# Projections of a graph-attention layer: from duos with seven products to trios with fifteen

## The chip, the cores and the metric

The kernel runs on one core of a Trainium2 chip (trn2). The metric is the time of one execution on the device, in microseconds (us). TensorE (PE) multiplies matrices and writes to PSUM; VectorE (DVE), ScalarE (ACT) and GpSimd (POOL) work on SBUF and PSUM; SyncE (SP) issues DMAs. Each engine runs its own instructions in order and waits on semaphores of the others.

## The reference

6250 nodes have 512 features each; 106250 edges, sorted by their destination, join them (self loops are among them). With eight heads of 64:

```python
Q, K, V = x @ Wq, x @ Wk, x @ Wv                       # 512 x 512 each
score = exp(clip(sum_d(K[src] * Q[dst]) / 8, -5, 5))   # per edge and head
h = x + segment_sum(V[src] * score, dst) / (segment_sum(score, dst) + 1e-6)
h = (h - mean(h, 0)) * rsqrt(var(h, 0) + 1e-5) * gamma + beta
out = layernorm(x + h)                                 # over the features
```

All in float32, output included.

## The kernel before, in words

The nodes lie in 49 tiles of 128 rows (the last is partly empty). Three stages follow one another. `project` computes Q, K and V of every tile and stores K and V side by side as rows of `kv_d`, and Q, split into a high and a low part, as rows of `q_d`. `attend` gathers the rows of `kv_d` by the edges' sources (indirect DMAs from POOL, line 751), multiplies them with Q, takes exponentials and sums by destination. `normalise` does the rest. Every gather needs all of `kv_d`: before its first one POOL waits for every store of K and V (`s_kva`, `s_kvb`).

Only `project` changes. Its core multiplies two tiles at a time (a duo): the product of the duo's x (two row blocks, the 512 inputs cut in two halves) with the weights (1536 columns cut in two halves of 768) is a product of 2 by 2 by 2 blocks, done in seven block products and sums (Strassen's method in Winograd's form). One block product is four `matmul` calls of 512 or 256 columns (the trace shows two MATMULs for one call). `product` on PE makes them (line 342); the sums of x blocks are made by DVE in `x_sums` (lines 480 to 485), those of the weights once in `weight_sums` (467 to 473); DVE and ACT decode the results out of PSUM (u2, u3, u4, kv_a, kv_b, c21; lines 590 to 616 and ACT's 435, 440). `split` (491, 493) makes the high part of Q with a scaling and the low part with a subtraction. There are 23 such duos (g = 0 to 22). The last duo's tiles (46, 47) and the 49th tile (`LONE`) are multiplied plainly (line 402: four `matmul` calls of 512 columns for one tile and one matrix, eight MATMULs in the trace); K and V of `LONE` come first of all (357, 374), its Q last.

What sets the order is written out by hand: every engine's list of instructions with its waits. `s_prod` counts finished products, `s_sums` the x sums, `s_wt` the weight sums, `s_split` the parts of Q. x is loaded three duos deep.

Besides, DVE computes tables of the edges piece by piece (`tables(n)`, one piece n after each of three places of a duo): pieces 0 to 6 count visits (497, 498), piece 20 releases POOL (`s_cnt`), pieces 21 to 27 make the digits (503), for each of which ACT writes a row (428). POOL, once released, adds beta to the 49 tiles of x: load (314), add (323, `xb`), store (331). At g = 12 PE transposes the source indices (365), and DVE copies them out (587).

## Time and profile before

| | us |
|---|---|
| median of 3 runs | 1910.76 (1909.86 to 1912.99) |
| the profiled execution | 1908.01 |
| its span | 1906.1 |
| PE / DVE / ACT / POOL busy in the span | 1861.6 / 1697.0 / 1367.5 / 1291.3 |
| PE's first product starts at | 10.47 |
| last copy of K and V ends at | 449.65 |
| first gather issued at | 452.53 |

The page shows the busy time of each engine in 40 slices of 47.65 us; `project` is the first nine and a half. TensorE's granted clock is shown per slice. The page's idle times name who ended the wait.

### The profile page before, as it was taken

The page shows a single profiled execution, that of the slowest core. Times are in us where ns is not written, and L with a number is a line of the kernel's source. Part 1 is how long each engine was busy: PE and PEld are TensorE (multiplying, and loading weights), DVE is VectorE, ACT ScalarE, POOL GpSimd, SP SyncE. Part 2 cuts the span into 40 slices and gives each one's busy share as a digit, 9 for nine tenths or more (in the row PEclk, how much of TensorE's full clock was granted, in tenths as well). Part 3 has the DMA queues.
Part 4 walks back from the last instruction along what each step waited for, and adds up shares of the span by engine and source line. Part 5 has one row for each costly group of instructions (what it writes and reads, how often), then busy time and mean ns, then how long its engine had stood idle before and what let it go on. Part 6 is the DMA issues. An engine that isn't in the chain of part 4 may idle for free.

```text
span 1906.1 us, 41424 instructions
## 1 busy us (share of the span) xinstructions
PE 1861.6 (98%) x7904; PEld 1362.2 (71%) x8014; DVE 1697.0 (89%) x2454; ACT 1367.5 (72%) x4602; POOL 1291.3 (68%) x1473
## 2 busy tenths in 40 slices
PE   7999999998999999999999999999999999999897
PEld 4555555554888888878888888888888888887333
DVE  6677755644999999999999999999999999999888
ACT  0002000002999999999999999999999999998857
POOL 0205666103777888788888888888888888885677
PEclk9999999999999999999999999999999999999999
DMA  5547788546999999999999999999999999999307
GB/s 183 162 151 250 288 319 274 186 161 231 357 358 356 362 367 358 346 351 368 368 356 353 352 366 369 354 355 355 366 361 358 360 355 365 370 358 370 122 33 287
DMA packets 184521, 589.09 MB, mean 309 GB/s; under 512 B 28480, under 2 KB 30240, under 8 KB 184480
## 3 DMA queue, kind: packets, MB, share of 16 engines
q0 software_dynamic: 135904, 465.14, 65.8%
q1 hardware_dynamic: 45120, 121.69, 17.8%
q10 hardware_dynamic: 3456, 1.78, 0.3%
q8 instruction: 18, 0.29, 0.1%
q14 instruction: 23, 0.19, 0.0%
HBM read 535.27 MB, written 78.91 MB: 322 GB/s over the span
## 4 chain that ended last, share of the span: by engine, by line
PE 74%; DVE 16%; issue 4%; DMA 4%; ACT 1%; POOL 1%; SPq 0%; DVEq 0%; ACTq 0%; POOLq 0%
PE acc L939 29%; PE places L342 22%; PE q_ps L923 17%; DVE kv L795 6%; DVE raw L806 5%; DMA kv<-kv_d,idx 2%; PE mm_ps L949 2%; PE banks L1151 1%; DVE stats L1288 1%; DVE agg L1281 1%; PE mm_ps L951 1%; PE places L402 1%; DMA q_tile<-xb_d 1%; POOL kv L751 1%; PE banks L1142 1%
## 5 line engine op out<-in xcount | busy, mean ns | idle before, releaser
L751 POOL DMA_INDIRECT kv<-kv_d,idx x880 | 887.0, 1008 | 339.2 <-issue 204.8
L846 ACT ACTIVATE kv<-kv 128x64 f32<-128x64 f32 x3520 | 889.0, 335 | 14.3
L939 PE MATMUL acc<-kv,mm_sb 128*128 128x260 f32 x3520 | 845.6, 383 | 4.1 <-POOL kv L714 2.2
L939 PEld LDWEIGHTS acc<-kv,mm_sb 128*128 128x128 f32 x3520 | 654.3, 190 | 137.9 <-issue 32.8
L923 PE MATMUL q_ps<-q_tile,mm_sb 128*128 x1760 | 559.2, 439 | 5.6 <-DVE kv L795 4.9
L795 DVE TENSOR_TENSOR kv<-q_ps,kv 128x1024 f32<-128x1024 f32 x440 | 536.1, 1218 | 14.0 <-PE q_ps L923 7.0
L806 DVE TENSOR_REDUCE raw<-kv 128x16 f32<-128x1024 f32 x440 | 532.2, 1210 | 0.0
L923 PEld LDWEIGHTS q_ps<-q_tile,mm_sb 128*128 128x128 f32 x1760 | 328.6, 189 | 74.4 <-DVE kv L795 20.8
L714 DVE TENSOR_TENSOR kv<-kv 128x384 f32<-128x384 f32 (+1 forms) x440 | 271.6, 617 | 0.1
L857 ACT ACTIVATE mm_sb<-mm_ps,less 128x1024 fp32r<-128x1024 f32 x220 | 241.2, 1096 | 13.1 <-remote 10.1
L435 ACT COPY p<-places 128x768 f32<-128x768 f32 x23 | 18.4, 798 | 243.5 <-PE places L342 243.5
L342 PE MATMUL places<-t_sb,s_sb 128*128 128x512 f32 (+1 forms) x552 | 185.6, 486 | 0.0
L342 PEld LDWEIGHTS places<-t_sb,s_sb 128*128 128x128 f32 x552 | 104.8, 190 | 73.7 <-issue 66.7
L714 POOL TENSOR_TENSOR kv<-kv 128x128 f32<-128x128 f32 x220 | 139.7, 635 | 14.2 <-ACT kv L861 9.1
L861 ACT ACTIVATE kv<-raw 128x16 f32<-128x16 f32 x440 | 91.1, 207 | 53.3 <-DVE raw L799 49.7
L342 PE MATMUL places<-w_sb,x_sb 128*128 128x512 f32 (+1 forms) x368 | 126.2, 486 | 0.0
L342 PEld LDWEIGHTS places<-w_sb,x_sb 128*128 128x128 f32 x368 | 69.9, 190 | 49.1 <-issue 44.5
L949 PEld LDWEIGHTS mm_ps<-nb,lb 128*128 128x128 bf16 x880 | 67.5, 98 | 34.8 <-issue 2.2
L590 DVE TENSOR_TENSOR u<-places,p 128x768 f32<-128x768 f32 x23 | 22.0, 957 | 75.5 <-PE places L342 75.5
L949 PE MATMUL mm_ps<-nb,lb 128*128 128x128 bf16 x880 | 85.1, 219 | 1.5 <-ACT mm_sb L857 1.5
L440 ACT COPY kv_a<-places 128x256 f32<-128x256 f32 x23 | 8.6, 372 | 103.3 <-DMA kv_d<-kv_a 51.8
L799 DVE TENSOR_SCALAR raw<-raw 128x16 f32<-128x16 f32 x440 | 78.9, 179 | 0.0
(171 smaller groups left out, 1358.6 us busy)
## 6 DMA issues: line engine op xcount, KB each, us to landing
q_tile<-q_d SPq DMA_DIRECT2D x49, 512.0 KB, 7.2
kv<-kv_d,idx POOLq DMA_INDIRECT x880, 6.2
kv_d<-kv_a SPq DMA_DIRECT2D x25, 512.0 KB, 5.5
xb<-in_x POOLq DMA_DIRECT2D x49, 256.0 KB, 4.3
xb_d<-xb POOLq DMA_DIRECT2D x49, 256.0 KB, 3.7
out_rows<-agg SPq DMA_DIRECT2D x49, 256.0 KB, 2.1
x_sb<-in_xT SPq DMA_DIRECT2D x24, 512.0 KB, 7.9
q_d<-q_a SPq DMA_DIRECT2D x24, 512.0 KB, 4.1
```

What stands on the lines that cost most here:

```text
L342: last = pe.matmul(out[:, cols], left[:, c, :], right[:, c, cols], start=fresh and c == 0, stop=c == DEEP - 1, skip_group_check=True)
L714: return eng.tensor_tensor(v, v, w, ALU.mult)
L751: pool.indirect_dma_start(kv[:, s, u, 0:2 * DIM], None, kv_d, bass.IndirectOffsetOnAxis(idx[:, s, u:u + 1], 0), bounds_check=N_NODES - 1, ...
L795: dve.tensor_tensor(k, q_ps[:, :, :], k, ALU.mult).then_inc(s_mul[s], 1)
L799: dve.tensor_scalar(raw[:, s1, :, :], raw[:, s1, :, :], -5.0, 5.0, ALU.max, ALU.min).then_inc(s_clip[s1], 1)
L806: dve.tensor_reduce(raw[:, s, :, :], heads(kv[:, s, :, 0:DIM]), AX.X, ALU.add).then_inc(s_red[s], 1)
L846: return act.activation(v, v, ACT.Copy, scale=kv[:, s, u, 2 * DIM + h:2 * DIM + h + 1])
L857: act.activation(mm_sb[:, sa // 2, :, :], mm_ps[:, :, :], ACT.Relu, bias=less[:, 0:1]).then_inc(s_mm[sa // 2], 1)
L861: act.activation(kv[:, s, :, 2 * DIM:KVW], raw[:, s, :, :], ACT.Exp).then_inc(s_exp[s], 1)
L923: last = pe.matmul(q_ps[:, u, :], one_hot(sb_, u, 1), part_q, start=(n == 0), stop=(n == 1))
L939: last = pe.matmul(acc[:, bass.ds(par, 1), DIM - (1 - n) * HALF:DIM + n * HALF], m, kv[:, sc, u, DIM + n * HALF:DIM + (n + 1) * HALF], sta ...
L949: pe.matmul(mm_ps[:, 0, n * P:(n + 1) * P], lb[:, sa + n // 2, n % 2 * P:(n % 2 + 1) * P], nb[:, :], start=True, stop=True)
```

## The change

`project` works on three tiles at a time (a trio; g = 0 to 15 covers 48 tiles). x has three row blocks and two halves of its inputs, and the weights have two halves of their inputs and three column blocks (K's 512 columns, Q's and V's): a 3 by 2 by 3 block product, done in fifteen products of 512 columns (two `matmul` calls each, line 367 of the new kernel) instead of eighteen. The numbering of sums and products (X9, T9, BANK_9 and so on) is by product. The weights need eleven sums of 1024 columns instead of four of 1536, x eleven of 256 columns for a trio instead of four for a duo, and the decoding fourteen instructions of 512 columns on DVE (counted by `s_dec`) and six copies on ACT (`s_kc`). The five buffers u2, u3, u4, p1, c21 become seven places `c_sb` (`held`); K and V of a tile are stored apart, as halves of a row. x is held two trios deep instead of three duos, the x sums once instead of twice. `LONE` is done whole at the start, in the order K, Q, V (line 375). The first loads are issued in turn: x of `LONE` and Wk, then, when the first half of Wk has landed, Wq, x of the first trio and Wv; POOL's first load (`dl`) waits for the same half. The first products wait for each half of a matrix. The transposes of the indices are at g = 8, the digits (pieces 21 to 27) come in trios 7, 8 and 9: three, three and one.

```diff
+                elif g > 1:
+                    sp.wait_ge(s_prod, made(g - 2, 15))
+                sp.dma_start(x_sb[:, g % 2, :, :, :],
...
+            sp.dma_start(x_sb[:, 1, 0, :, :], xT[LONE]).then_inc(s_x[1], 16)
+            load_w(wk, 0, s_wk)
+            sp.wait_ge(s_wk[0], 16)
+            load_w(wq, 1, s_wq)
+            load(0)
+            load_w(wv, 2, s_wv)
             sp.wait_ge(s_kc, 1)
-            sp.dma_start(kv_d[LONE * P:(LONE + 1) * P, :], kv_a[:, :]).then_inc(s_kva, 16)
...
+            load(1)
...
+                if 0 < g < TRIOS - 1:
+                    load(g + 1)
...
+                a, b, c = 3 * g, 3 * g + 1, 3 * g + 2
+                sp.wait_ge(s_kc, copied(g, 4))
+                store_k(c, k_out(2), s_kva)
+                sp.wait_ge(s_dec, decoded(g, 3))
+                store_v(b, v_out(1), s_kvb)
+                store_q(a, split_of(g, 0), q_a, s_qa)
+                sp.wait_ge(s_dec, decoded(g, 7))
+                store_k(a, k_out(0), s_kva)
+                sp.wait_ge(s_dec, decoded(g, 8))
+                store_k(b, k_out(1), s_kva)
+                sp.wait_ge(s_dec, decoded(g, 11))
+                store_v(a, v_out(0), s_kvb)
+                sp.wait_ge(s_dec, decoded(g, 12))
+                store_v(c, v_out(2), s_kvb)
+                store_q(b, split_of(g, 1), q_b, s_qb)
+                store_q(c, split_of(g, 2), q_c, s_qc)
...
-            pool.dma_start(dl[:, :], dlast.broadcast_to([P, BLOCKS_IN])).then_inc(s_dl, 16)
...
+            pool.wait_ge(s_wk[0], 16)
+            pool.dma_start(dl[:, :], dlast.broadcast_to([P, BLOCKS_IN])).then_inc(s_dl, 16)
...
+                    last = pe.matmul(place(bank), left[:, c, :], right[:, c, :], start=fresh and c == 0,
+                                     stop=c == DEEP - 1, skip_group_check=True)
...
-                    pe.wait_ge(s_c22, g)
+                    pe.wait_ge(s_dec, decoded(g - 1, 14))
...
+                pe.wait_ge(s_x[g % 2], trio_x(g))
+                if g:
+                    pe.wait_ge(s_kc, copied(g - 1, 4))
+                product(BANK_5, a_part(g, 2, 0), weight(B00), True)
+                pe.wait_ge(s_sums, summed(g, X9))
+                wait(pe, s_dec, decoded(g - 1, 7))
+                first_wait(g, 2)
+                product(BANK_9, x_sum(X9), weight(T9), True)
+                pe.wait_ge(s_sums, summed(g, X2))
+                wait(pe, s_dec, decoded(g - 1, 8))
+                first_wait(g, 3)
+                product(BANK_2, x_sum(X2), weight(T2), True)
+                pe.wait_ge(s_kc, copied(g, 1))
...
+                pe.wait_ge(s_kc, copied(g, 2))
+                pe.wait_ge(s_sums, summed(g, X10))
+                first_wait(g, 4)
+                product(BANK_9, x_sum(X10), weight(T10), False)
...
+                pe.wait_ge(s_dec, decoded(g, 1))
+                first_wait(g, 7)
+                product(BANK_9, a_part(g, 0, 1), weight(T14), False)
...
                 if g == 0:
...
+                pe.wait_ge(s_sums, summed(g, X8))
+                pe.wait_ge(s_kc, copied(g, 6))
+                first_wait(g, 11)
+                product(BANK_1, x_sum(X8), weight(T8), False)
+                pe.wait_ge(s_sums, summed(g, X7))
+                wait(pe, s_dec, decoded(g - 1, 14))
+                if g == 0:
+                    pe.wait_ge(s_split, 2)
+                product(BANK_7, x_sum(X7), weight(B11), True)
...
+                wait(act, s_dec, decoded(g - 1, 8))
+                act.copy(held(M5), place(BANK_5)).then_inc(s_kc, 1)
+                act.wait_ge(s_prod, made(g, 2))
+                wait(act, s_dec, decoded(g - 1, 14))
+                act.copy(held(M9), place(BANK_9)).then_inc(s_kc, 1)
...
+                for landed in (*s_wk, *s_wq):
+                    dve.wait_ge(landed, 16)
+                dve.tensor_tensor(weight(T0), weight(B00), weight(B01), ALU.subtract).then_inc(s_wt, 1)
+                dve.wait_ge(s_prod, 2)
...
+                dve.tensor_tensor(weight(T1), weight(B02), weight(T0), ALU.subtract).then_inc(s_wt, 1)
+                dve.tensor_tensor(weight(T6), weight(B12), weight(T0), ALU.subtract).then_inc(s_wt, 1)
+                dve.tensor_tensor(weight(T8), weight(B11), weight(T13), ALU.add).then_inc(s_wt, 1)
+
+            def x_sums_first(g):
+                dve.wait_ge(s_x[g % 2], trio_x(g))
+                if g:
+                    dve.wait_ge(s_prod, made(g - 1, 6))
+                dve.tensor_tensor(x_sum(X9), a_part(g, 0, 0), a_part(g, 2, 0), ALU.add).then_inc(s_sums, 1)
+                dve.tensor_tensor(x_sum(X2), a_part(g, 1, 0), a_part(g, 2, 0), ALU.add).then_inc(s_sums, 1)
+                dve.wait_ge(s_sums, summed(g, X9))
+                dve.tensor_tensor(x_sum(X10), x_sum(X9), a_part(g, 0, 1), ALU.add).then_inc(s_sums, 1)
+                dve.wait_ge(s_sums, summed(g, X2))
+                dve.tensor_tensor(x_sum(X4), x_sum(X2), a_part(g, 1, 1), ALU.add).then_inc(s_sums, 1)
...
-            for g in range(LAST):
-                if g == TABLE_DUO:
+            x_sums_third(0)
+            x_sums_last(0)
+            dve.wait_ge(s_prod, 2)
+            split(q_c, place(BANK_7), 1, s_qc, 0)
+            for g in range(TRIOS):
...
+                dve.tensor_tensor(held(T), place(BANK_9), held(M5), ALU.subtract).then_inc(s_dec, 1)
...
+                dve.tensor_tensor(held(U), place(BANK_2), held(M5), ALU.add).then_inc(s_dec, 1)
                 tables(3 * g)
-                dve.wait_ge(s_prod, made(g, 3))
-                split(q_a, place(g, 0)[:, 0:DIM], 2 * g + 1, s_qa, 16 * g)
-                dve.wait_ge(s_prod, made(g, 4))
-                dve.wait_ge(s_u, 3 * g + 1)
-                dve.tensor_tensor(u3[:, :], place(g, 2)[:, 0:SIDE], u2[:, :], ALU.add).then_inc(s_u, 1)
-                if g + 1 < LAST:
-                    x_sums(g + 1)
+                dve.wait_ge(s_prod, made(g, 7))
+                dve.wait_ge(s_kvb, 16 * (1 + 3 * g))
+                dve.wait_ge(s_dec, decoded(g, 2))
+                dve.wait_ge(s_kc, copied(g, 5))
+                dve.tensor_tensor(v_out(1), place(BANK_13), held(U), ALU.subtract).then_inc(s_dec, 1)
+                dve.tensor_tensor(held(M13), held(M13), held(M9), ALU.add).then_inc(s_dec, 1)
+                dve.wait_ge(s_prod, made(g, 8))
+                dve.tensor_tensor(held(T), held(T), place(BANK_0), ALU.subtract).then_inc(s_dec, 1)
+                dve.wait_ge(s_dec, decoded(g, 5))
+                dve.tensor_tensor(held(M9), held(M9), held(T), ALU.subtract).then_inc(s_dec, 1)
+                split(q_a, held(T), split_of(g, 0), s_qa, 16 * g)
+                if g + 1 < TRIOS:
+                    x_sums_first(g + 1)
+                dve.wait_ge(s_prod, made(g, 9))
+                dve.wait_ge(s_kc, copied(g, 4))
+                dve.tensor_tensor(k_out(0), place(BANK_9), held(M5), ALU.subtract).then_inc(s_dec, 1)
...
                 tables(3 * g + 1)
...
+                if g + 1 < TRIOS:
+                    x_sums_second(g + 1)
+                dve.wait_ge(s_kc, copied(g, 6))
+                dve.tensor_tensor(held(M1), held(M1), held(M2), ALU.add).then_inc(s_dec, 1)
+                dve.tensor_tensor(held(M2), held(M2), v_out(1), ALU.add).then_inc(s_dec, 1)
+                dve.wait_ge(s_prod, made(g, 12))
+                dve.wait_ge(s_dec, decoded(g, 9))
+                dve.tensor_tensor(v_out(0), place(BANK_0), held(M1), ALU.add).then_inc(s_dec, 1)
+                dve.wait_ge(s_prod, made(g, 13))
+                dve.wait_ge(s_dec, decoded(g, 10))
+                dve.tensor_tensor(v_out(2), place(BANK_3), held(M2), ALU.subtract).then_inc(s_dec, 1)
                 tables(3 * g + 2)
...
+                dve.wait_ge(s_prod, made(g, 14))
+                dve.tensor_tensor(held(M13), place(BANK_1), held(M13), ALU.subtract).then_inc(s_dec, 1)
+                dve.wait_ge(s_dec, decoded(g, 13))
+                split(q_b, held(M13), split_of(g, 1), s_qb, 16 * g)
+                if g + 1 < TRIOS:
+                    x_sums_third(g + 1)
+                dve.wait_ge(s_prod, made(g, 15))
+                dve.wait_ge(s_split, 2 * split_of(g, 0))
+                dve.tensor_tensor(held(T), place(BANK_7), held(M9), ALU.add).then_inc(s_dec, 1)
+                dve.wait_ge(s_dec, decoded(g, 14))
+                split(q_c, held(T), split_of(g, 2), s_qc, 16 * (g + 1))
+                if g + 1 < TRIOS:
+                    x_sums_last(g + 1)
...
-            pool.wait_ge(soft["s_kva"], 16 * (TILES // 2 + 1))
-            pool.wait_ge(soft["s_kvb"], 16 * (TILES // 2 + 1))
+            pool.wait_ge(soft["s_kva"], 16 * TILES)
+            pool.wait_ge(soft["s_kvb"], 16 * TILES)
```

What DVE executes just before the copy of the transposed indices (the last row), from the decoding of c21 in duo 11 on; u3 and u4 are sums decoded into SBUF:

```order
L608 TENSOR_TENSOR c21<-u3,places 128x512 [waits s_prod]
L609 TENSOR_TENSOR kv_b<-u3,places 128x256
L491 TENSOR_SCALAR q_b<-c21 128x512 [waits s_qb,s_c21]
L493 SCALAR_TENSOR_TENSOR q_b<-c21,q_b 128x512 [waits s_split]
L616 TENSOR_TENSOR kv_a<-places,u4 128x768 [waits s_u,s_kva,s_prod]
L587 CAST src_t<-places 128x896 [waits s_tr]
```

And now, from the splitting of the second tile's Q in trio 7 on (`places` is PSUM, `c_sb`, `q_b`, `q_c`, `s_sb`, `x_sb` are SBUF):

```order
L565 TENSOR_SCALAR q_b<-c_sb 128x512 [waits s_qb,s_dec]
L567 SCALAR_TENSOR_TENSOR q_b<-c_sb,q_b 128x512 [waits s_split]
L551 TENSOR_TENSOR s_sb<-s_sb,x_sb 128x256 [waits s_sums,s_prod]
L552 TENSOR_TENSOR s_sb<-x_sb,s_sb 128x256
L553 TENSOR_TENSOR s_sb<-s_sb,x_sb 128x256
L554 TENSOR_TENSOR s_sb<-x_sb,s_sb 128x256
L714 TENSOR_TENSOR c_sb<-places,c_sb 128x512 [waits s_split,s_prod]
L565 TENSOR_SCALAR q_c<-c_sb 128x512 [waits s_qc,s_dec]
L567 SCALAR_TENSOR_TENSOR q_c<-c_sb,q_c 128x512 [waits s_split]
L559 TENSOR_TENSOR s_sb<-s_sb,x_sb 128x256 [waits s_prod]
L666 CAST src_t<-places 128x896 [waits s_tr]
```

Nine of the ten rows before the copy read SBUF alone, where two of five did. L714 is the last of the trio's fourteen decoding instructions, which the transposes of the next trio wait for.

PE around the transposes, before:

```order
L342 MATMUL places<-w_sb,s_sb 128x512
L342 MATMUL places<-w_sb,s_sb 128x256
L365 MATMUL places<-ident,kv 128x128 [waits s_c22,s_visit]
L365 MATMUL places<-ident,kv 128x128 x6
L342 MATMUL places<-w_sb,x_sb 128x512 [waits s_u,s_x0]
```

and now:

```order
L367 MATMUL places<-w_sb,s_sb 128x512 [waits s_dec,s_sums]
L367 MATMUL places<-w_sb,s_sb 128x512
L392 MATMUL places<-ident,kv 128x128 [waits s_dec,s_visit]
L392 MATMUL places<-ident,kv 128x128 x6
L367 MATMUL places<-w_sb,x_sb 128x512 [waits s_kc,s_x0]
L367 MATMUL places<-w_sb,x_sb 128x512
L367 MATMUL places<-w_sb,s_sb 128x512 [waits s_dec,s_sums]
```

The transposes waited for a result decoded after the fifth of the duo's seven products (`s_c22`); now they wait for the one decoded after the last of fifteen.

## Rows read from the trace of the kernel before

**Rows 1.** TensorE's granted clock in the page's 40 slices (tenths of full speed).

```profile
PEclk9999999999999999999999999999999999999999
```

**Rows 2.** The chain of waits to 460 us: start us, us, what.

```profile
10.47 5.17 PE places L357 x8
...
18.22 3.43 PE places L374 x8
21.66 214.14 PE places L342 x664
235.80 0.77 PE places L365 x7
236.56 198.73 PE places L342 x616
435.29 13.75 PE places L402 x32
...
449.06 0.59 ACT kv_b L450
...
459.18 10.32 DMA kv<-kv_d,idx
```

**Rows 3.** Timeline of DVE at the start: start us, us, line, shapes, idle before.

```profile
8.73 0.23 DVE L577 CAST iota_row<-iota_i 128x128 f32<-128x128 int32 x1 [6.50 <-DMA kv<-in_dlast]
...
9.71 1.02 DVE L581 TENSOR_TENSOR kv<-kv 128x832 f32<-128x832 int32 x1
...
13.94 0.42 DVE L483 TENSOR_TENSOR s_sb<-x_sb 128x256 f32<-128x256 f32 x1
14.28 0.42 DVE L485 TENSOR_TENSOR s_sb<-x_sb,s_sb 128x256 f32<-128x256 f32 x1
...
17.63 1.76 DVE L469 TENSOR_TENSOR t_sb<-w_sb,t_sb 128x1536 f32<-128x1536 f32 x1
```

**Rows 4.** Timeline of DVE in duo 22, when POOL is quiet.

```profile
432.75 0.69 DVE L608 TENSOR_TENSOR c<-u,places 128x512 f32<-128x512 f32 x1 [0.76 <-PE places L342]
433.35 0.41 DVE L609 TENSOR_TENSOR kv_b<-u,places 128x256 f32<-128x256 f32 x1
433.68 0.42 DVE L491 TENSOR_SCALAR q_b<-c 128x512 fp32r<-128x512 f32 x1
434.14 0.69 DVE L493 SCALAR_TENSOR_TENSOR q_b<-c,q_b 128x512 fp32r<-128x512 f32 x1
```

**Rows 5.** Groups by shape, DVE, 150 to 340 us: busy us, mean ns.

```profile
L493 DVE SCALAR_TENSOR_TENSOR q_b<-c,q_b 128x512 fp32r<-128x512 f32 x10 | 15.0, 1499 | 0.3
...
L483 DVE TENSOR_TENSOR s_sb<-x_sb 128x256 f32<-128x256 f32 x11 | 10.0, 909 | 0.0
...
L482 DVE TENSOR_TENSOR s_sb<-s_sb,x_sb 128x256 f32<-128x256 f32 x11 | 9.3, 842 | 0.4
...
L491 DVE TENSOR_SCALAR q_b<-c 128x512 fp32r<-128x512 f32 x10 | 6.4, 642 | 0.0
L480 DVE TENSOR_TENSOR s_sb<-x_sb 128x256 f32<-128x256 f32 x11 | 6.2, 567 | 0.0
```

**Rows 6.** Timeline of DVE and POOL at 272 us.

```profile
271.78 2.48 DVE L493 SCALAR_TENSOR_TENSOR q_b<-c,q_b 128x512 fp32r<-128x512 f32 x1
...
272.41 1.29 POOL L323 TENSOR_TENSOR xb<-xb,bet 128x512 f32<-128x512 f32 x1
```

**Rows 7.** Groups by shape, POOL, 150 to 350 us.

```profile
L323 POOL TENSOR_TENSOR xb<-xb,bet 128x512 f32<-128x512 f32 x49 | 63.1, 1287 | 4.4 <-DMA xb<-in_x 3.9
```

**Rows 8.** Groups by shape, DVE, 20 to 435 us: the digits.

```profile
L503 DVE TENSOR_SCALAR kv<-kv 128x1024 int32<-128x1024 int32 x7 | 5.5, 788 | 0.0
```

**Rows 9.** DMA issues of x from 234 and from 288 us: KB, us to landing.

```profile
x_sb<-in_xT SPq DMA_DIRECT2D x1, 512.0 KB, 9.6
...
x_sb<-in_xT SPq DMA_DIRECT2D x1, 512.0 KB, 13.2
```

**Rows 10.** Timeline at the first gather.

```profile
452.53 1.07 POOL L751 DMA_INDIRECT kv<-kv_d,idx  x1 [104.09 <-DMA kv_d<-kv_b]
```

More of the change, by code:

```diff
@@ L338, in _, with product @@
         def _(pe):
-            def product(out, left, right, fresh=True, told=True):
+            def product(bank, left, right, fresh):
                 for c in range(DEEP):
-                    for cols in (slice(0, DIM), slice(DIM, SIDE)):
-                        last = pe.matmul(out[:, cols], left[:, c, :], right[:, c, cols], start=fresh and c == 0,
-                                         stop=c == DEEP - 1, skip_group_check=True)
-                if told:
-                    last.then_inc(s_prod, 1)
@@ L347, in by_sum @@
-            def by_sum(g, n, k):
-                pe.wait_ge(s_sums, 4 * g + k)
-                wait(pe, s_wt, k if g == 0 else 0)
-                product(place(g, n), s_sb[:, g % 2, k - 1, :, :], t_sb[:, k - 1, :, :])
-            pe.wait_ge(s_x[X_DUOS - 1], 16)
-            lone = x_sb[:, X_DUOS - 1, 0, :, :]
-            pe.wait_ge(s_wk, 16 * CHUNKS)
-            for c in range(CHUNKS):
-                pe.matmul(place(-1, 5)[:, 0:DIM], lone[:, c, :], w_sb[:, c, DIM:2 * DIM], start=c == 0,
-                          stop=c == CHUNKS - 1)
@@ L387, in _ @@
+                first_wait(g, 10)
+                product(BANK_0, x_sum(X6), weight(T6), False)
+                pe.wait_ge(s_sums, summed(g, X3))
+                wait(pe, s_dec, decoded(g - 1, 12))
                 if g == 0:
                     pe.wait_ge(s_kc, 1)
[L389 to L394 removed]
@@ L395, in _ @@
-                pe.wait_ge(s_u, 3 * g + 1)
-                pe.wait_ge(s_sums, 4 * g + 4)
-                product(place(g, 5), s_sb[:, g % 2, 3, :, :], b_part(1, 1))
-            def plain(out, left, n):
-                for c in range(CHUNKS):
-                    last = pe.matmul(out, left[:, c, :], w_sb[:, c, n * DIM:(n + 1) * DIM], start=c == 0,
-                                     stop=c == CHUNKS - 1)
-                return last
-            a, b = (x_sb[:, LAST % X_DUOS, n, :, :] for n in range(2))
```

368 lines of the change are left out of this document (176 added, 192 removed).

## The prediction

> **What bounds the kernel now.** I read the chain of waits first. Up to 449.06 us it is TensorE (PE) alone: K of `LONE` from 10.47 us, then 83 block products in 214.14 us, the transposes in 0.77 us, 77 products in 198.73 us and the plain products in 13.75 us, with no gap that anyone else made [rows 2]. The granted clock is full in all slices [rows 1]. So `project` is as long as PE's columns take, and what counts is the moment at which the last part of K and V leaves PSUM: ACT's copy from 449.06 to 449.65 us. POOL's first gather starts at 452.53 us [rows 10], 2.9 us behind it, and the chain's first step that isn't PE's is a gather, 459.18 to 469.50 us [rows 2]. What follows (three quarters of the time) has the same instructions in both kernels; I take it as shifted as a whole by the shift of that moment. PE's own Q products behind it, three of 3.43 us before and two of 1.72 now, lie beside the stores and the gathers, and the chain doesn't run through them; so I count their saving as nothing (bounds: half of the 6.9 us gained, 2 us lost if the last stores of Q, closer to the gathers now, hold them up).
>
> The second reading is DVE's. Its instructions that read only SBUF take longer while POOL adds beta. The low part of Q takes 0.69 us when POOL is quiet [rows 4], and 1.50 us on average between 150 and 340 us [rows 5]; one of them, 2.48 us long, started 0.63 us before an addition of POOL's and ended 0.56 us behind it [rows 6]. POOL makes 49 additions of 1.29 us, none of which shows a delay on average [rows 7]. What reads PSUM isn't touched.
>
> **PE's work and the start.** A block product of 1536 columns takes 214.14 / 83 = 2.58 us, a plain one of 2048 takes 3.43 us [rows 2]; so one of 1024 takes 1.72 us, and a trio 15 x 1.72 = 25.8 us (8.6 us a tile, against 9.03). The first eight MATMULs took 5.17 us, 1.74 more than the later eight, after 10.5 us without work and at a granted clock shown as full [rows 1, 2]. I keep that. When PE starts is not in the trace: the first half of Wk now has 0.75 MB ahead of it or with it, where Wk shared the queues with 3 MB. At half of what was needed before I take 4.8 us (bounds 4 and 8, the latter near the old 10.47 less the time of half a matrix). Then K, Q and V of `LONE` end at 4.8 + 5.17 + 3.43 + 3.43 = 16.8, eight products of trio 0 at 30.6 us. The ninth needs DVE's first decoding, which stands behind all weight sums. DVE's path: `dl` lands perhaps at 10.5 (it landed at 8.73 with its first use) and its tables take 2.0 us; x of the trio at 12; six x sums of 0.34 [rows 3] to 14.2; eleven weight sums of 1.76 x 2/3 = 1.17 us to 27.1; five x sums to 28.8; the split of Q of `LONE` 1.4 to 30.2; the decoding 0.7: 30.9 us [rows 3, 4]. PE waits 0.3 us. From there 230 products remain to the one that ends V (trio 0 has 7 left, 15 trios have 225, and the last two come behind V): 230 x 1.72 = 395.6, the transposes 0.8, DVE's subtraction and its signal 0.8: K and V would be out at 428.1 us. Against 449.65 that is 21.5 us less. If the loads are later by 3 us, DVE's path makes it 3 less.
>
> **What DVE gives back.** After product 7 and ACT's copy of it, 12.8 us into the trio, DVE has in order, up to the last decoding (the one after product 15): eight decodings that read PSUM at 0.60, four that don't at 0.60, two splits at 0.46 + 0.60, ten x sums at 0.34, together 12.7, and 0.4 where one waits for the one before [rows 3, 4]. That ends at 25.9, on the heels of product 15. In trio 7 two digits stand in it, 0.7 each [rows 8]: DVE is 1.5 us late. That much I am sure of.
>
> POOL's additions come on top. Piece 20 of the tables releases POOL; it stands in trio 6, at about 16.8 + 6 x 25.8 + 13 x 1.72 = 194 us, where in duo 6 it came at some 145 (21.7 + 6 x 18.1 + 5 x 2.6 and the pieces): 50 us later. The 49 additions, all between 150 and 350 us before [rows 7], move with it, to the middle of trio 7 and up to trio 14, and still end 40 us ahead of the gathers. Their price on DVE before: (1.499 - 0.69) x 10 + (0.909 - 0.42) x 11 + (0.842 - 0.42) x 11 + (0.642 - 0.42) x 10 + (0.567 - 0.42) x 11 = 22 us [rows 5], on SBUF-only instructions that would have needed 10.5 duos x 2.8 us = 29 us: 0.75 us for each. In the stretch above the change has 4 x 0.69 + 2 x 1.11 + 10 x 0.42 = 9.2 us of these, against 2.8 in a duo. By that ratio 6.9 us is added. The bounds: at the rate per time of the window before, 22 / 190 x 14.5 = 1.7 us; and every addition of POOL that falls in (one in 4 us, 5.5 of them) at the largest single delay, 1.79 us: 9.9 us. I take 6.9, since it follows how often the two meet.
>
> **The Trainium skill** (page "SBUF — State Buffer", section "SBUF: two separate sides") says that a DVE instruction with two SBUF inputs and a GpSimd instruction that reads SBUF exclude each other, and that the one which starts first holds the port to its end. The first half fits the rows; the second would let DVE finish in the case above, where it had started first and all the same ended behind POOL. By it about half of the delays would go.
>
> Who waits: PE's transposes before trio 8 now stand behind the last decoding of trio 7, so all of the lateness, 1.5 + 6.9 = 8.4 us (3.2 to 11.4), shows as PE idle. In other trios PE can do four products first: product 5 needs ACT's copy M9, which needs that decoding, so 6.9 - 0.7 = 6.2 us of lateness are hidden. Trio 8 (two digits in the stretch) shows 2.2 us; trios 9 to 13, 7.0 us late, 0.8 each, 4.0: together 6.2 (0 to 12). After the long wait PE's first products may be slow as the first of all were: 1.7 (0 to 3.5). The sum given back is 16.3 us (3 to 27).
>
> **Sum.** 21.5 - 16.3 = 5.2 us less: 1908.0 - 5.2 = 1902.8 for the profiled execution, which lies 2.75 us under the median shown; so 1905.5.
>
> Costed at nothing, with their cover: the extra stores (nine DMA issues a trio on SP, with nothing behind them but the next x); ACT's six copies, 3.6 us in 25.8; SP's wait for the digits' rows at g = 13: POOL writes them at its 37th tile, by my shift near 350 us, and SP comes at 16.8 + 13 x 25.8 + what is given back, 365 or so (if little is given back, it waits a few us; nothing needs its stores for as long).
>
> **Rivals.** B, DVE's lateness stays small: POOL and DVE meet as rarely per time as before (1.7 us a trio), nothing but 3.2 us before trio 8 and 1.7 of slow products. Then 21.5 - 4.9 = 16.6 less: 1894. For it: POOL will find other pauses; against it: the SBUF-only work per time doubles. By the page's rule half of the 6.9 goes: 5.0 + 1.7 given back, 14.8 less, 1896; the row at 271.78 speaks against it, I give it 0.05 inside B's 0.25.
>
> C, slower: x comes late. It is held two trios deep, its load can be issued only after product 15 and, in SP's order, after the last Q store, some 2 us on plus DVE's lateness; DVE needs it 2 us after product 8, at about 16. With 8.4 - 1.4 of lateness the load leaves at 9 to 10 and has some 6 to 7 us, or more as far as DVE itself is late. 512 KB took 9.6 us in the busy window and 13.2 beside POOL's digit stores [rows 9]; now it is 768 KB, with less queued ahead. If it takes 12 to 13 us, each of the seven loaded trios adds 1 to 2 us, as DVE's wait feeds its own lateness: 10 us. Then 5 us more: 1915.5. It decides from about 10.5 us of landing time on.
>
> D, the shift of K and V is lost behind something in `attend`: nothing in the rows holds the gathers but K and V; 0.05, 1910.
>
> **Chances.** Forecast A 0.50, B 0.25, C 0.20, D 0.05. A alone ranges from 1899 to 1912. The range 1893 to 1915.5 leaves out about 2 in 10. 0.2% is 3.8 us, about what a measurement of this kernel tells from none: faster means below 1907.0. A gives 0.27 to faster, 0.20 to no change, 0.03 to slower; B all to faster; C 0.03 to no change and 0.17 to slower; D to no change. Faster 0.52, same 0.28, slower 0.20.
>
> **What would show it.** PE's first product near 5 us and `LONE` whole by 17; products of 1.72 us, trios of 25.8 where PE doesn't wait; an idle time of PE of about 8 us before the transposes, ended by DVE; some 6 us in front of fifth products, ended by ACT, in trios 9 to 13; SBUF-only instructions of DVE lengthened by 5 to 7 us a trio between 205 and 400 us; the last V out near 444 us. Waits of DVE for x would show C; a trio 7 without a wait, B. I am wrong in the mechanism if PE waits elsewhere, or if the gathers start at the old time after V is out early.

## The result and the profile after

| | before | changed |
|---|---|---|
| median, 20 runs each (us) | 1910.31 (1906.21 to 1913.39) | 1921.18 (1911.71 to 1928.57) |
| ratio, 95% interval | | 1.0057 (1.0045 to 1.0069) |
| the profiled execution / its span | 1908.01 / 1906.1 | 1917.64 / 1915.9 |
| K and V out of PSUM | 449.65 [rows 2] | 459.0 |
| first gather issued | 452.53 [rows 10] | 461.85 |

The change makes the kernel 0.57% slower; 1905.5 was forecast, with 1915.5 as the upper end. From the moment at which K and V are out, both kernels need the same: span less that moment is 1456.4 us before and 1456.9 after. So the loss lies in `project`. In the two profiled executions it is 9.4 us, where V out (the moment at which the last part of V is out of PSUM) was forecast at 444.4 and came at 459.0: 14.6 us are to be explained. (The one of the changed kernel lies 3.5 us under its median; its times also spread over 17 us, those of before over 7.)

TensorE's busy time and granted clock in 40 slices of the span, the changed kernel; before, the clock showed 9 (90% or more) in all of them [rows 1]:

```profile
PE   8999789998999999999999999999999999999897
PEclk9999989999999999999999999999999999999999
```

The fifth slice (192 to 239 us) has the low share of work, the sixth (239 to 287 us) the low clock: just ahead of the transposes, and from them to the waits of trio 9. TensorE's timeline at the start and there: start us, us, engine, line, what, and in brackets the idle time before and what ended it.

```profile
5.34 5.49 PE L375 MATMUL places<-w_sb,x_sb 128*128 128x512 f32 x8 [5.34 <-DMA w_sb<-in_wk]
12.68 3.70 PE L375 MATMUL places<-w_sb,x_sb 128*128 128x512 f32 x8 [1.84 <-DMA w_sb<-in_wq]
17.48 3.70 PE L375 MATMUL places<-w_sb,x_sb 128*128 128x512 f32 x8 [1.09 <-DMA w_sb<-in_wv]
21.02 1.88 PE L367 MATMUL places<-w_sb,x_sb 128*128 128x512 f32 x4
...
46.95 1.88 PE L367 MATMUL places<-w_sb,x_sb 128*128 128x512 f32 x4
...
54.25 7.13 PE L367 MATMUL places<-w_sb,s_sb 128*128 128x512 f32 x16 [0.26 <-ACT c_sb L478]
...
241.60 1.73 PE L392 MATMUL places<-ident,kv 128*128 128x128 f32 x7 [13.71 <-DVE c_sb L714]
243.12 2.59 PE L367 MATMUL places<-w_sb,x_sb 128*128 128x512 f32 x4
...
269.58 1.88 PE L367 MATMUL places<-w_sb,x_sb 128*128 128x512 f32 x4
271.30 3.60 PE L367 MATMUL places<-w_sb,s_sb 128*128 128x512 f32 x8
277.64 2.81 PE L367 MATMUL places<-w_sb,x_sb 128*128 128x512 f32 x4 [2.75 <-ACT c_sb L475]
283.04 10.03 PE L367 MATMUL places<-w_sb,s_sb 128*128 128x512 f32 x16 [2.59 <-ACT c_sb L478]
```

`LONE` and trio 0 start late; from 73.23 us on trios run at 25.75 us each, and up to trio 7 no wait is over 0.3 us; the transposes wait 13.71 us for DVE's last decoding; trio 9 waits twice, 5.3 us together, and its next 16 MATMULs take 10.03 us where 16 took 7.03. Behind these stand one wait of 1.38 and one of 0.21 us, so that from the transposes on TensorE idles 20.6 us in all. The answer to [rows 6] is DVE and POOL just ahead of the transposes:

```profile
218.39 2.08 DVE L683 TENSOR_TENSOR c_sb<-c_sb 128x512 f32<-128x512 f32 x1
220.39 0.41 DVE L565 TENSOR_SCALAR q_a<-c_sb 128x512 fp32r<-128x512 f32 x1
220.84 2.48 DVE L567 SCALAR_TENSOR_TENSOR q_a<-c_sb,q_a 128x512 fp32r<-128x512 f32 x1
223.24 0.41 DVE L534 TENSOR_TENSOR s_sb<-x_sb 128x256 f32<-128x256 f32 x1
223.58 0.41 DVE L535 TENSOR_TENSOR s_sb<-x_sb 128x256 f32<-128x256 f32 x1
223.91 1.82 DVE L537 TENSOR_TENSOR s_sb<-s_sb,x_sb 128x256 f32<-128x256 f32 x1
```

```profile
218.63 1.28 POOL L349 TENSOR_TENSOR xb<-xb,bet 128x512 f32<-128x512 f32 x1
...
221.48 1.28 POOL L349 TENSOR_TENSOR xb<-xb,bet 128x512 f32<-128x512 f32 x1
...
224.16 1.28 POOL L349 TENSOR_TENSOR xb<-xb,bet 128x512 f32<-128x512 f32 x1
```

An addition comes every 2.7 to 2.9 us (once 3.5), ten of them from 215.95 to 241.30. Each of these three meets one DVE instruction that had already started (218.39, 220.84, 223.91), and that one ends 0.56, 0.56 and 0.29 us behind the addition: its own length less a tenth. Nine of the ten meet DVE before the decoding that the transposes wait for (240.78, which reads PSUM and keeps 0.68 us). Each of them lengthens one instruction by 0.86 to 1.79 us, two digits among them (1.54 and 1.74 instead of 0.68), together by 11.6 us. POOL's stay at 1.28 us, and between them stand only the issues of a store and a load.

### The profile page after: what moved, and what is told of

It reads as the page before. It is cut to its first block, busy times and chain, and to the rows that moved or that the text cites. A ratio compares the mean times of both kernels' runs of the same rounds, so it can differ in the third digit from the quotient of the medians.

```text
span 1915.9 us, 41086 instructions
## 1 busy us (share of the span) xinstructions
PE 1846.1 (96%) x7637; PEld 1288.4 (67%) x7638; DVE 1760.5 (92%) x2608; ACT 1395.8 (73%) x4650; POOL 1296.9 (68%) x1473
## 4 chain that ended last, share of the span: by engine, by line
PE 66%; DVE 20%; DMA 5%; issue 5%; ACT 2%; POOL 1%; ACTq 0%; POOLq 0%; DVEq 0%; SPq 0%
PE acc L1036 29%; PE places L367 17%; PE q_ps L1020 16%; DVE kv L891 5%; DVE raw L902 4%; DMA kv<-kv_d,idx 4%; PE mm_ps L1046 2%; PE mm_ps L1048 2%; DVE stats L1385 1%; DVE agg L1369 1%; ACT kv L942 1%; DVE agg L1378 1%; DMA q_tile<-xb_d 1%; POOL kv L847 1%; DVE kv L809 1%
## 5 line engine op out<-in xcount | busy, mean ns | idle before, releaser
L942 ACT ACTIVATE kv<-kv 128x64 f32<-128x64 f32 x3520 | 889.1, 335 | 14.3
L891 DVE TENSOR_TENSOR kv<-q_ps,kv 128x1024 f32<-128x1024 f32 x440 | 536.2, 1219 | 16.8 <-DMA kv<-kv_d,idx 8.9
L367 PE MATMUL places<-w_sb,s_sb 128*128 128x512 f32 x704 | 313.3, 597 | 4.4 <-ACT c_sb L478 4.4
L367 PEld LDWEIGHTS places<-w_sb,s_sb 128*128 128x128 f32 x704 | 134.5, 192 | 176.8 <-issue 164.2
L367 PE MATMUL places<-w_sb,x_sb 128*128 128x512 f32 x256 | 119.4, 599 | 2.8 <-ACT c_sb L475 2.8
L475 ACT COPY c_sb<-places 128x512 f32<-128x512 f32 x16 | 9.4, 585 | 114.6 <-PE places L367 106.6
L367 PEld LDWEIGHTS places<-w_sb,x_sb 128*128 128x128 f32 x256 | 48.9, 192 | 64.5 <-issue 56.9
L1048 PE MATMUL mm_ps<-lb,nb 128*128 128x512 bf16 x220 | 83.6, 380 | 0.0
L493 ACT COPY c_sb<-places 128x512 f32<-128x512 f32 x16 | 9.4, 586 | 98.7 <-PE places L367 98.7
```

What stands on the lines that cost most here:

```text
L367: last = pe.matmul(place(bank), left[:, c, :], right[:, c, :], start=fresh and c == 0, stop=c == DEEP - 1, skip_group_check=True)
L891: dve.tensor_tensor(k, q_ps[:, :, :], k, ALU.mult).then_inc(s_mul[s], 1)
L942: return act.activation(v, v, ACT.Copy, scale=kv[:, s, u, 2 * DIM + h:2 * DIM + h + 1])
L1048: last = pe.matmul(mm_ps[:, 1, :], nb[:, :], lb[:, sa:sa + 2, :], start=True, stop=True)
```

## The experiments

Ten kernels in three groups (e1 to e4, e5 to e8, e9 and e10), each on one chip and timed against the kernel before there. On the first group's chip `attend` is slower (before takes 2106.2 us), so there the ratios and the moments within `project` count. "V out" is the end of DVE's last subtraction of V (459.0 us in the changed kernel), from one execution's trace each. It differs from the ratio by that execution's distance from the median and by the start: with the same start code, trio 0 begins at 21.02 us in the changed kernel and between 18.95 and 19.22 in e3, e6, e9 and e10. Theory A: DVE is late because its SBUF-only work collides with POOL's additions, and TensorE pays where no other product can be done meanwhile, above all before the transposes. Rival C of the prediction, a late x, is looked for in each trace too.

### Take the additions' reading away: e1_iota, e2_before_iota

```diff
-pool.tensor_tensor(xb[:, n, :], xb[:, n, :], bet[:, :], ALU.add).then_inc(s_xb, 1)
+pool.iota(bet[:, :].bitcast(I32), pattern=[[1, DIM]], base=0, channel_multiplier=0)
+pool.iota(busy[:, :], pattern=[[1, DIM]], base=0, channel_multiplier=0).then_inc(s_xb, 1)
```

The same edit in the changed kernel and in the kernel before; the loads, the stores and their order stay.

> The changed kernel, with POOL's addition of beta replaced by two instructions of the same total length or nearly (1.1 us) that only write (what is left out: beta, so the output is another one). POOL's DMAs stay, a little denser. Theory, contention: the 13.7 us wait before the transposes falls to 1 to 3 us, the waits before products 4 and 5 of trios 9 and 10 vanish, V's last subtraction ends near 435 us instead of 459, the time is about 1898 us, some 12 us under the kernel before. Rival, work: DVE is late by its own greater work and the digits; then at most 8 us go, V is out after 450, the time is 1912 or more. SBUF-only instructions of DVE keep 0.41 and 0.69 us in the first case.

> The kernel before with the same replacement of POOL's addition (beta left out). Theory: the lengthened instructions of DVE cost nothing there, since PE never waited; V out at 449.7, the time within 3 us of the kernel before. Rival: contention costs before too, somewhere else than in projections: 4 us or more less.

Measured: e1_iota 0.9941 (0.9928 to 0.9955), V out at 436.0, idle before the transposes 2.77 us, none in trios 9 to 13. e2_before_iota 1.0012 (1.0003 to 1.0021): the kernel before gains nothing. Its V is out at 452.05 where 449.7 was expected; TensorE starts 0.6 us later there and waits once, 1.35 us. The windows 100 to 430 us of the changed kernel and of e1_iota (columns: busy us and instructions of each engine, granted clock, DMA share, GB/s):

```profile
100.00:430.00 330.00, 309.37 (x713) 136.28 (x712) 248.54 (x403) 49.21 (x79) 132.31 (x166) 0.96 0.69 231
```

```profile
100.00:430.00 330.00, 327.23 (x765) 145.02 (x764) 218.88 (x424) 52.85 (x84) 124.90 (x214) 0.99 0.70 238
```

DVE does 21 instructions more in 30 us less, at an equal DMA rate. By V out, which `attend` doesn't touch, the additions cost the changed kernel 23 us, and the ratio of the old one shows no gain. A is shown in its main part, and so is what the trios are worth without the collision: 0.6%. POOL is nearly as busy (124.90 against 132.31 us), so what went is its reading and not its presence.

### Move the transposes: e3_late_tr

```diff
-                if g == TABLE_TRIO:          # at the start of trio 8
-                    ... transposes
                 ...
                 product(BANK_0, x_sum(X0), weight(T0), True)
+                if g == TABLE_TRIO:          # before product 9 of trio 8
+                    ... transposes; DVE's copy of them moves likewise
```

> The changed kernel with the transposes of trio 8 moved from ahead of product 1 to ahead of product 9, and DVE's copy of them behind the x sums (all is computed). Theory A, DVE is the bound from the middle of trio 7 to trio 9: the wait of 13.7 us turns into one of some 7.5 before product 5 of trio 8, and the rest comes back before trio 9's products 4 and 5; in all 0 to 4 us gained. Rival, the place of the wait is the price: PE has four more products to do beside the late DVE and the 6 us so hidden stay gained, plus the slow products after a long idle time: 7 to 9 us.

Measured: 1.0009 (0.9997 to 1.0021) against the change's 1.0057 (1.0059 for e4_at_once on the same chip), so 10 us gained by the place of one wait; V out at 444.0, in an execution 4.3 us under the median. Theory A had let the lateness show at the next wait (0 to 4 us gained); that part of it falls, and the rival is the nearer one. TensorE's timeline in it:

```profile
234.82 3.46 PE L367 MATMUL places<-w_sb,x_sb 128*128 128x512 f32 x4 [3.38 <-ACT c_sb L475]
240.31 8.83 PE L367 MATMUL places<-w_sb,s_sb 128*128 128x512 f32 x16 [2.03 <-ACT c_sb L478]
248.98 0.93 PE L422 MATMUL places<-ident,kv 128*128 128x128 f32 x7
249.74 3.60 PE L367 MATMUL places<-w_sb,x_sb 128*128 128x512 f32 x8
253.18 3.60 PE L367 MATMUL places<-w_sb,s_sb 128*128 128x512 f32 x8
257.99 4.53 PE L367 MATMUL places<-w_sb,s_sb 128*128 128x512 f32 x10 [1.22 <-DVE src_t L686]
```

In trio 8, 6.6 us in three waits stand instead of 13.71 us: products that need nothing of DVE's last decodings lie ahead of each. With what comes behind, TensorE idles 8.9 us instead of 20.6.

### The order of the first loads: e4_at_once

```diff
-            pool.wait_ge(s_wk[0], 16)
-            sp.wait_ge(s_wk[0], 16)
```

> The changed kernel with its first loads issued at once, as before (SP and POOL don't wait for the first half of Wk; all is computed). Theory: PE starts some 3 to 4 us later, but has no waits for Wq and Wv; product 1 of trio 0 starts within 1.5 us of the 21.0 us it had, and the time is the same within 2 us. Rival: the staggering gains what it seems to gain at the first product, 4 us; or it costs (the later landing of x, dl and Wv is on DVE's path), and at once is 2 to 4 us faster.

Measured: 1.0059 (1.0045 to 1.0072), the same as the change; V out 457.15. TensorE starts at 5.23 us, where 3 to 4 us later than 5.34 was expected. It waits 0.78 us for the second half of Wk and 0.67 for Wv, and trio 0 begins at 19.31 us; in e3_late_tr, on the same chip with the loads in turn, it begins at 19.22. Issuing the loads in turn neither gives nor costs anything that these runs can tell. This trace is also a second look at the free-running additions: 11.16 us of idle time before the transposes and 10.5 behind them, where the changed kernel's has 13.71 and 6.9. How the loss splits between the two places changes from one execution to the next.

### Move the additions: e5_paced, e8_paced_busy

```diff
+            for first in range(0, TILES, XB_RING):        # four at a time
+                g = 3 + first // XB_RING
+                ... wait for the loads of all four
+                pool.wait_ge(s_prod, made(g, 1))          # e8_paced_busy: made(g, 7)
+                ... four additions, then four stores (behind trio 10's also those of the digits), then four loads
```

All arithmetic is done, and the count is the same: 49 additions.

> The changed kernel with all of its arithmetic. POOL's 49 additions of beta no longer run free (49 of them between 216 and 385 us, one per 3.5 us, wherever VectorE stands); they come four at a time, once per trio in trios 3 to 15, after the trio's product 1, where VectorE is idle for 4.9 us. Four additions of 1.28 us are 5.1 us. Theory A (an addition costs time only where it falls on VectorE's SBUF-only work): last V subtraction about 436 us, as with the additions taken out (436.0), TensorE's idle time before the transposes about 2.8 us, no idle time above 1 us in trios 9 to 13, ratio to the kernel before 0.993 to 0.996. Rival R1 (the additions cost through their DMAs and SBUF traffic in general, not through VectorE): last V subtraction 450 or later, ratio above 1.002.

> The same paced additions, four per trio in trios 3 to 15, but started at the end of the trio's product 7, where VectorE has 8.7 us of work without a gap: same number, same rate, same DMAs, only another place in the trio. Theory A: each trio's VectorE work ends 4 to 5 us later; in an ordinary trio the 4.9 us that VectorE idles before product 5 take most of that, in trio 7 the transposes wait for it: idle time there 7 to 8 us, last V subtraction 441 to 448 us, ratio 0.997 to 1.001. Rival R2 (the lower rate alone is the cure, the place does not matter): as e5_paced, 436 us. Rival R1 (traffic in general): as e5_paced, 450 us or later.

Measured: e5_paced 0.9932 (0.9917 to 0.9948), V out at 437.15, 1.1 us behind what e1_iota let expect; e8_paced_busy 0.9958 (0.9941 to 0.9974), V out at 443.6, in its range, the ratio a little below its own. R1 (traffic in general) is refuted: the traffic is there in both. The two differ by 6.4 us of V out, while the intervals of their ratios overlap. The lower rate and the bunching alone, in the worse place, give 15.4 of the 21.9 us, so R2 holds for the larger part. A burst of POOL's in e5_paced (one row), DVE beside it, and then DVE in e8_paced_busy beside a burst from 214.95 to 220.80:

```profile
261.50 5.77 POOL L354 TENSOR_TENSOR xb<-xb,bet 128x512 f32<-128x512 f32 x4 [13.04 <-PE places L378]
```

```profile
261.78 1.27 DVE L576 TENSOR_SCALAR q_c<-c_sb 128x512 fp32r<-128x512 f32 x1
263.09 1.64 DVE L578 SCALAR_TENSOR_TENSOR q_c<-c_sb,q_c 128x512 fp32r<-128x512 f32 x1
264.65 1.49 DVE L570 TENSOR_TENSOR s_sb<-s_sb,x_sb 128x256 f32<-128x256 f32 x1
268.22 0.69 DVE L681 TENSOR_TENSOR c_sb<-places,c_sb 128x512 f32<-128x512 f32 x1 [2.08 <-PE places L378]
```

```profile
216.17 0.69 DVE L689 TENSOR_TENSOR kv<-places,c_sb 128x512 f32<-128x512 f32 x1 [1.78 <-ACT c_sb L501]
216.78 1.22 DVE L690 TENSOR_TENSOR c_sb<-c_sb 128x512 f32<-128x512 f32 x1
217.91 0.68 DVE L692 TENSOR_TENSOR c_sb<-c_sb,places 128x512 f32<-128x512 f32 x1
218.62 1.05 DVE L694 TENSOR_TENSOR c_sb<-c_sb 128x512 f32<-128x512 f32 x1
219.59 1.48 DVE L576 TENSOR_SCALAR q_a<-c_sb 128x512 fp32r<-128x512 f32 x1
```

The four of e5_paced lengthen three instructions by 2.9 us (4.40 against 0.43 + 0.69 + 0.42), and 2.08 us of idle time behind them are still left: free of charge. That isn't so in all trios: the burst at 205.77 us of e5_paced meets three x sums of the trio before, and TensorE waits 0.72 us at M9 of trio 7, as it does 1.53 us in trio 5. In e8_paced_busy a burst adds 1.9 us (3.75 against 0.69 + 0.69 + 0.43), since its start falls on DVE's own wait for ACT. Run free, nine additions added 11.6. So e8_paced_busy lengthens DVE's work less than e5_paced, and TensorE still waits longer before the transposes (3.99 us, where 7 to 8 were expected, against 2.29): what it adds stands ahead of the decodings that TensorE waits for. There a delay's place counts for more than its size. With slower transposes and a slower product behind the wait (1.73 and 2.79 us against 0.95 and 1.88) the place is worth 3.4 us in these two executions.

The rest of the 6.4 us is mostly something else, rival C's late x. In e8_paced_busy:

```profile
307.31 7.40 POOL L364 DMA_DIRECT2D lb_d<-kv  x8
...
334.24 1.02 DVE L545 TENSOR_TENSOR s_sb<-x_sb 128x256 f32<-128x256 f32 x1 [5.11 <-DMA x_sb<-in_xT]
...
348.21 8.83 PE L378 MATMUL places<-w_sb,s_sb 128*128 128x512 f32 x16 [2.59 <-ACT c_sb L489]
```

POOL stores the digits (`lb_d`) just ahead of SP's load of x at 316.46 us. That load lands 17.8 us later, where the one that follows the digits in e5_paced takes 8.4; DVE waits 5.11 us for it, and TensorE loses 0.43 + 2.59 us of waiting and 1.8 us by slow MATMULs. Whether the burst's place or chance brings the two DMAs together here, no run tells.

### Move the digits: e6_digits

```diff
-                return [BITS - 1 - (n - 21)] if 21 <= n < 21 + BITS else []
+                return [BITS - 1 - DIGITS.index(n)] if n in DIGITS else []   # (21, 22, 24, 25, 27, 28, 30)
```

> The changed kernel with only the seven binary digits moved: to the first and second of the three table places of a trio (trios 7 to 10), none in the third. ScalarE's doubling of a digit then never stands before the next trio's copy of product 1 (M5) while VectorE is late. Theory D (that order cost the wait of 2.75 us in trio 9 by itself): that wait goes, last V subtraction 455 to 456.5 us instead of 459.0, ratio to the kernel before 1.003 to 1.005. Rival (VectorE is late anyway, so the next wait, for the copy of M9, grows by what the first one loses): 458 to 459.5 us, ratio 1.005 to 1.007.

Measured: 1.0051 (1.0031 to 1.0071). The wait for M5 is gone, the one for M9 has taken its place. ACT in the changed kernel, and then in e6_digits:

```profile
275.97 1.15 ACT L466 ACTIVATE kv<-kv,minus 128x1024 bf16<-128x1024 int32 x1 [4.94 <-DVE kv L577]
277.03 0.57 ACT L475 COPY c_sb<-places 128x512 f32<-128x512 f32 x1
282.40 0.59 ACT L478 COPY c_sb<-places 128x512 f32<-128x512 f32 x1 [4.81 <-DVE c_sb L714]
```

```profile
276.36 0.59 ACT L479 COPY c_sb<-places 128x512 f32<-128x512 f32 x1 [8.55 <-DVE c_sb L715]
```

In the first, ACT's copy of M5 stood ready and waited behind the doubling of a digit that DVE hadn't made; TensorE lost 2.75 us. In the second TensorE loses 5.07 us at M9 in one piece, about the 5.3 of the two waits before. The rival's mechanism is seen, and theory D's isn't; the ratio's interval holds both of their ranges. V out was 464.7, outside both ranges, in an execution 3.6 us above the median. Late x is seen there: one load of x lands 14.3 us after its issue, DVE waits 4.96 us for it at 352.04, and TensorE then waits 5.14 us and takes 10.13 us for 16 MATMULs.

### Both moves: e7_paced_late_tr

The edits of e5_paced and e3_late_tr together.

> The paced additions together with the transposes moved from the start of trio 8 to before its product 9; all of the arithmetic is done. Theory A: what is left of the wait before the transposes (about 2.8 us) goes too, since VectorE's last step of trio 7 now has four products' time; last V subtraction 433 to 435 us, ratio 0.992 to 0.995. Rival (the wait only moves to src_t, as the 1.22 us seen before it): 435 to 437 us, equal to the paced version alone.

Measured: 0.9907 (0.9890 to 0.9924), 1890.97 us beside 1910.28 for the kernel before on this chip; V out at 433.4. Between 213 and 332 us TensorE is busy all the time:

```profile
213.00:243.00 30.00, 30.00 (x72) 13.21 (x71) 19.26 (x37) 8.46 (x11) 10.38 (x13) 1.00 0.88 266
243.00:269.00 26.00, 26.00 (x67) 11.90 (x66) 21.17 (x35) 6.69 (x9) 10.16 (x12) 1.00 0.71 241
269.00:305.00 36.00, 36.00 (x85) 15.96 (x84) 28.28 (x50) 4.25 (x8) 20.21 (x25) 1.00 0.80 258
305.00:332.00 27.00, 27.00 (x64) 11.97 (x63) 16.46 (x32) 3.51 (x6) 9.27 (x12) 1.00 0.90 312
```

It does all of the arithmetic and is the fastest version here, 0.9% below the kernel before and a little below the range expected. By V out it is 3.75 us better than e5_paced, as theory A had it; the ratios' intervals overlap.

### Which part of the loss is the wait before the transposes: e9_after_tr

```diff
-DIGITS_AT = 36
+DIGITS_AT = 28
...
             pool.wait_ge(s_bet, 16)
+            pool.wait_ge(s_tr, 1)
```

> The changed kernel; POOL's additions of beta, free-running as in it, start only when the transposes of trio 8 are done (and the digits go out to DRAM after addition 28 instead of 36, so that SyncE does not wait for them in trio 13). Nothing is left out. Ten additions fewer fall into trio 7, all 49 fall into the trios from 8 on. Theory A (a wait that costs is the one before the transposes, plus the decodings that are late in trios 8 to 13): the wait before the transposes is 2 to 3 us instead of 13.71, last V subtraction 446 to 450 us instead of 459.0, ratio to the kernel before 0.999 to 1.002. Rival (the time is only paid later, since ten more additions press on the trios behind): 455 to 459 us, ratio 1.004 to 1.006.

Measured: 0.9986 (0.9975 to 0.9997), just below the range expected; V out at 451.1, 1.1 us above its range. The wait before the transposes is 2.29 us. Behind it stand five waits of 1.25 to 3.63 us, 11.9 together (6.9 in the changed kernel). So the additions ahead of the transposes cost 11.4 us there, about the 11.6 by which they lengthened DVE's work. The rival's range (1.004 to 1.006) is missed by far: little of it is paid later. Of the 5 us more behind the transposes, 4.2 (waits of 2.96 and 1.25 us) stand behind two waits of DVE for x (4.44 and 1.12 us); the first of these loads lands 13.7 us after its issue, beside the digit stores that this edit moved. That the moved additions cost anything there isn't shown.

### Does idle time slow what follows: e10_warm

```diff
+                    for _ in range(6):       # product 1's operands, into BANK_5, not told to anyone
+                        for c in range(DEEP):
+                            pe.matmul(place(BANK_5), ..., start=c == 0, ...)
                     pe.wait_ge(s_visit, 3)
```

> The changed kernel; before TensorE waits for the transposes it runs six extra products (24 MATMULs of 512 columns, 10.3 us) into a PSUM bank whose content the next product overwrites; nothing else is changed and nothing is left out. They lie inside its idle time of 13.71 us. Theory C (the idle time itself slows what follows: transposes 1.73 instead of 0.77 us, first product 2.59 instead of 1.88 us, granted clock 0.94 in the trio behind): transposes take 0.8 us, the product behind them 1.8 us, last V subtraction 1.5 to 2 us earlier than 459, and about 4 us earlier if the slow stretch of trio 9 hangs on it too; ratio 1.003 to 1.005. Rival (the slow clock comes from something else, such as the load on VectorE and the DMAs): transposes and products as in the changed kernel, ratio 1.005 to 1.007.

Measured: 1.0041 (1.0029 to 1.0053), in theory C's range, while its interval overlaps the change's (1.0045 to 1.0069); V out at 454.4. TensorE there:

```profile
226.13 10.46 PE L393 MATMUL places<-w_sb,x_sb 128*128 128x512 f32 x24
238.02 0.95 PE L398 MATMUL places<-ident,kv 128*128 128x128 f32 x7 [1.43 <-DVE c_sb L720]
238.81 1.88 PE L367 MATMUL places<-w_sb,x_sb 128*128 128x512 f32 x4
...
274.06 3.51 PE L367 MATMUL places<-w_sb,x_sb 128*128 128x512 f32 x4 [4.19 <-ACT c_sb L481]
279.47 8.83 PE L367 MATMUL places<-w_sb,s_sb 128*128 128x512 f32 x16 [1.89 <-ACT c_sb L484]
```

With work in place of idle time the transposes take 0.95 instead of 1.73 us and the product behind them 1.88 instead of 2.59, while DVE and the DMAs are as loaded as before: theory C of this experiment. That is 1.5 us; the other 3.1 of the 4.6 by which V is out earlier aren't the clock's, since the transposes start at 238.02 instead of 241.60 (trio 0 had begun 1.9 us earlier). The product behind the idle time that is left, in trio 9, is slow here too (3.51).

## Why the prediction was wrong

**The start, 16.8 us for `LONE`: 4.2 us too early.** TensorE's first product came at 5.34 us (4.8 expected), but Wq and Wv landed late by 1.84 and 1.09 us. I had let the three matrices follow without a wait and argued only the first. They are 2.9 of the 4.2; 0.5 is the first product, 0.7 the length of the three. Of this about 2 us is this one execution's: with the same code e3, e6, e9 and e10 are at 18.95 to 19.22. DVE's path was as late, since x of the trio came at 16.04 instead of 12: weight sums 1.14 us apart (1.17 forecast), and a first decoding that ends at 34.78 (30.9 forecast), with no wait of TensorE's behind it.

**Products of 1.72 us, trios of 25.8 us:** right (25.75 us, from 73.23 us on). The gain of the trios is real; e1_iota, e5_paced and e7_paced_late_tr keep it.

**The wait before the transposes, 8.4 us: 13.71.** Place, releaser and cause were right; the size of the term "6.9 from POOL's additions" was not. With no addition in that stretch 2.3 to 2.8 us stay (e1_iota, e5_paced, e9_after_tr; I had 1.5), so they cost 10.9 to 11.4 us. The 0.75 us per us of SBUF-only work [rows 5] was an average over a window in which an addition came every 4 us. I took that average as given. But before, too, they mostly came 2.7 to 3.4 us apart, with pauses of 6 to 7 us in between (the additions at 167.26 and 173.04 us are 5.8 apart, as POOL waits 3.07 us for a store of `xb`); in trio 7 no such pause fell into the stretch. And since each delay makes the stretch longer, more of them fall in: nine, where my upper bound had 5.5. That bound (9.9 us) was too low for this reason. An estimate from the rows: the stretch from 213.70 to 228.18 us of e9_after_tr, undisturbed, is 14.5 us; with 1.29 us added every 2.82 us it becomes 14.5 / (1 - 1.29 / 2.82) = 26.7, and 25.9 were measured (215.56 to 241.46). The ratio depended on how both engines keep step, and it was carried over as if it were a constant.

**Trios 8 to 13, 6.2 us of idle time: 6.9 us** (2.75, 2.59, 1.38, 0.21), in trios 9, 10 and 13. The tolerance of four products was right in kind; the wait at M5, behind ACT's doubling of a digit, wasn't foreseen, but e6_digits shows it to be the same lateness. **Slow products after long idle time, 1.7 us:** 1.7 at the transposes (1.73 - 0.77 and 2.59 - 1.88), as expected, but I counted it once; it came again in trio 9, with 3.0 us for 16 MATMULs (10.03 against 7.03) and 0.9 for the product before them. So the step that failed is the sum given back, 16.3 us, and in it first the 6.9 for POOL's additions, which cost about 11, then the slow products, counted once. With 5.3 us more at the transposes, about 5 more behind them, most of it the slow clock, and the start's 4.2 the 14.6 us are found. This is the account of one execution; the traces of e4_at_once and e6_digits, where the additions run free as well, idle 11.16 and 9.84 us before the transposes and 10.5 and 13.9 behind them.

**Handover, nothing:** right; behind V out all is shifted rigidly, which refutes D. **C:** x of a trio (768 KB) landed in 5.0 to 9.3 us in the changed kernel's trace, where more than 10.5 was its condition, and DVE never waited for it behind trio 0: the right sign by the wrong mechanism. But its mechanism is real, for one load in a trace and not in seven trios: beside POOL's digit stores one load of x took 13.7 to 17.8 us in e4, e6, e8 and e9, DVE waited 4.4 to 5.2 us for it, and TensorE then 1.4 to 5.1 (in e1 and e3 it took 13.6 and 12.8 us, and DVE waited 0.99 and 2.25). The prediction's row of 13.2 us beside the digit stores [rows 9] pointed at it. **B:** refuted; its condition is brought about by e5_paced, at 1897.26 us.

**The Trainium skill** (page "SBUF — State Buffer", section "SBUF: two separate sides"): its first half, exclusion between a two-input SBUF instruction of DVE and a GpSimd one, agrees with e1_iota. Its second, that the one that starts first holds the port to its end, isn't what these rows show: at 218.39, 220.84 and 223.91 us DVE started first and ended last. The doubt I had about it was right.

What stays open: why the clock fell so far in trio 9 and hardly after some waits of the same length; what part of bunching's gain is the lower rate and what the bunch, since no version spaced single additions evenly over all trios; and how much of the changed kernel's median is late x, since its one trace has none and no version moved only the digit stores.

## What to carry to other kernels

When two engines collide on a resource, the cost is set by how often they meet, and that changes when one of them is sped up or made busier. So bound it by the fastest rate at which the other can go, in a stretch that the delays themselves make longer. Ask of each delay where it can be hidden: here the same 49 additions cost 23 us of V out run free, 8 bunched in a busy stretch (nearly 5 of these are the late x), and 1 where DVE mostly had idle time (each against e1_iota). A wait for another engine's last result belongs where some products that don't need it are still to be done. And moving one engine's work moves its DMAs too: look at what they meet.

## What the runs showed of the hardware

- A DVE instruction that reads only SBUF and meets a POOL addition ends behind it by about its own length, even if it began up to 0.64 us earlier (218.39 us: 2.08 instead of 0.69). It holds for one input too: 1.27 instead of 0.43 at 261.78 us. POOL pays only in a bunch: four additions take 5.77 us beside DVE and 4.94 alone.
- POOL's `iota`, which only writes, doesn't delay DVE's low part of Q (0.69 us in e1_iota, 1.88 on average in the changed kernel for `q_a`); the high part took 0.52 to 0.57 us beside it, against 0.43 undisturbed.
- After idle time TensorE's granted clock is lower: 0.75 on average between 283 and 295 us of the changed kernel, a mean of full speed (2.4 GHz) and the lower level (1.2 GHz), after waits of 2.75 and 2.59 us, and full again from 295. The length of the wait alone doesn't decide it: behind 2.29 us of idle time the product after the transposes took 2.88 us in e9_after_tr and 1.88 in e5_paced.
- A load of x (768 KB) that lands in 5.0 to 7.2 us in the changed kernel up to 290 us takes 13.7 to 17.8 us beside POOL's eight digit stores (e9_after_tr, e6_digits, e4_at_once, e8_paced_busy).
- With free-running additions the time spreads more: the changed kernel over 17 us in 20 runs, e6_digits over 14 in 7; e5_paced over 5.3 in 6, e7_paced_late_tr over 4.4 in 5. Whether the additions or the late x make it spread isn't shown.
